# Payload scatters that wait for every batch of four (16 in the edge sums) to have landed

## The chip, the cores and the metric

One core of a Trainium2 chip runs the whole program in one launch. The metric is the device time in microseconds, the median of several executions without a profiler. The profile is one more execution of the same program, recorded by the hardware profiler.

## What is computed

Four blocks are applied one after the other to 6250 nodes with 256 features; each adds its result to its input. The edges are a list of pairs (source, destination).

```python
x = x + gnn0(layernorm(x), edges, edge_attr_32)   # mean of relu(attr @ W_time) over the edges of a node, dense adapter
x = x + ffn0(layernorm(x))                        # router, 6 experts of 3 layers, the best 2 per node
x = x + gnn1(layernorm(x), edges)                 # 2 layers of graph attention, 106250 edges
x = x + ffn1(layernorm(x), ffn_edges)             # router by graph attention (131072 edges), 4 experts, the best 2
```

The graph attention of a layer is

```python
e = leaky_relu(el[src] + er[dst]); ex = exp(e - segment_max(e, dst)[dst])
out = segment_sum(hp[src] * (ex / segment_sum(ex, dst)[dst])[:, None], dst)
```

## The kernel before

The program is a row of stages, each a method with a block of its own; a stage begins when all engines have left the one before. In order: `setup`, `sorts`, `edge_sums`, `norm_T`, `adapter`, `ln_stats`, `norm_T`, `router0`, `gates`, `experts`, `ln_stats`, then twice `gat_tables` and `attention`, then `finish`, `ln_stats`, `norm_T`, `router_tables`, `attention`, `last_experts`.

`sorts` works out for every edge at which place it stands once the edges are grouped by destination, and writes the edge attributes to these places in DRAM (`attr_sorted`, L274: 832 indirect DMAs from GpSimd). Of two further lists it keeps the places (`pos`) and a payload of 16 bytes per edge (`pay`) in SBUF: 832 columns of 128 edges for list 1 and 1024 for list 2. These payloads must stand sorted in DRAM (`pay_sorted`) before the `attention` that reads them back. One indirect DMA of GpSimd (a scatter, L449) writes one column: 128 rows of 16 bytes, each to its own place. That makes 1856 scatters.

They are not a stage of their own. They are shared out over the stages between `sorts` and the attentions, where GpSimd has nothing else to do: each stage gets a list `scatter=[(list, first column, end)]`, and its GpSimd program consists of `scatter_pool` for that list and nothing more. The counts, in order of the stages:

| Stage | Scatters |
|---|---|
| edge_sums | 384 |
| norm_T (three times) | 56 each |
| adapter | 148 |
| ln_stats (three times) | 24 each |
| router0 | 56 |
| gates | 14 |
| experts | 94 of list 1, then 560 of list 2 |
| gat_tables (twice) | 104 each |
| finish | 68 |
| router_tables | 84 |

In `scatter_pool` (L437 to L455) the scatters go out in batches of `AHEAD` = 16 that count their landings on two semaphores in turn. Before a batch, GpSimd waits until the batch before last has landed, so that up to 32 scatters are under way and the batch just issued may still be landing. At the end it waits for both semaphores. Every stage has its own pair, and no other engine waits for a scatter: what it holds up is the end of its stage, and so the start of the next.

The gathers of `attention` (L790: 928 for each of the first two, 1216 for the third) are indirect DMAs of GpSimd too. Before the gathers of a group, GpSimd waits for `s_U`, TensorE's count of finished groups.

Of the kernel before, what the change touches and what calls it, by code (L numbers as in the profile page):

```python
# [49 lines left out]
STEP = 7  # L50
RING = 8
DRING = 8
AHEAD = 16
SLOPE = 0.2
BIG = 2.0 ** 100
NX0, NX1 = 6, 4
# [27 lines left out]
class Kernel:  # L84
# [345 lines left out]
                self.stats(dve, c, st, dl, var, s_var, s_std)  # L430


    def scatter_slots(self, sem, g, lo, hi):

        return dict(g=g, lo=lo, hi=hi, done=sem.pool(2))

    def scatter_pool(self, pool, s):  # L437


        g, lo, hi, done = s["g"], s["lo"], s["hi"], s["done"]  # L440
        out = self.pay_sorted[g]
        last = pool.to_reg(out.shape[0] - 1)
        issued = [0, 0]
        for n in range(hi - lo):
            j = n // AHEAD % 2
            if n % AHEAD == 0 and issued[j]:
                pool.wait_ge(done[j], 16 * issued[j])
            issued[j] += 1
            pool.indirect_dma_start(  # L449
                out=out, out_offset=bass.IndirectOffsetOnAxis(ap=self.pos[g][:, lo + n:lo + n + 1], axis=0),  # L450
                in_=self.pay[g][:, lo + n, :], in_offset=None,
                bounds_check=last, oob_is_err=False).then_inc(done[j], 16)
        for j in range(2):
            if issued[j]:
                pool.wait_ge(done[j], 16 * issued[j])  # L455


    def stats(self, dve, c, st, dl, var, s_var, s_std):
# [1772 lines left out]
def program(nc, ins, out):  # L2231
    i = ins
    with ExitStack() as keep:
        k = Kernel(nc, ins, out)
        k.setup(keep)
        k.sorts()
        with nc.sbuf_tensor("acc0", [P, NB, AD + 1], F32) as acc0:
            k.edge_sums(acc0, scatter=[(1, 0, 384)])
            with nc.sbuf_tensor("XT0", [P, KT, NB * P], F32) as XT:
                k.norm_T(XT, scatter=[(1, 384, 440)])  # L2240
                k.adapter(XT, acc0, scatter=[(1, 440, 588)])
        k.ln_stats(scatter=[(1, 588, 612)])
        with nc.sbuf_tensor("XT1", [P, KT, NB * P], F32) as XT, nc.sbuf_tensor("LG0", [P, NB, NX0], F32) as LG, \
                nc.sbuf_tensor("g0", [P, NB, NX0], F32) as g:
            k.norm_T(XT, scatter=[(1, 612, 668)])
            k.router0(XT, LG, scatter=[(1, 668, 724)])
            k.gates(LG, g, NX0, True, scatter=[(1, 724, 738)])
            k.experts(XT, g, [(i["L0_ffn_expert_w1"], i["L0_ffn_expert_b1"], ACT.Relu),
                              (i["L0_ffn_expert_w2"], i["L0_ffn_expert_b2"], ACT.Relu),
                              (i["L0_ffn_expert_w3"], i["L0_ffn_expert_b3"])], NX0, scatter=[(1, 738, ET), (2, 0, 560)])  # L2250
        k.ln_stats(scatter=[(2, 560, 584)])
        with nc.sbuf_tensor("acc1", [P, NB, D + 1], F32) as acc, nc.sbuf_tensor("m1", [P, NB, 1], F32) as m, \
                nc.sbuf_tensor("adst1", [P, NB, 1], F32) as adst:
            for layer in range(2):
                k.gat_tables(layer, acc, m, adst, scatter=[(2, 584 + 104 * layer, 688 + 104 * layer)])
                k.attention(1, 1, D + 1, k.tab_gat, acc, m, adst)
            k.finish(acc, i["L1_gnn_bias"][1:2, :], scatter=[(2, 792, 860)])
        k.ln_stats(scatter=[(2, 860, 884)])
        with nc.sbuf_tensor("XT2", [P, KT, NB * P], F32) as XT:
            k.norm_T(XT, scatter=[(2, 884, 940)])  # L2260
            with nc.sbuf_tensor("acc2", [P, NB, 3 * HEADS * FH1], F32) as acc, \
                    nc.sbuf_tensor("m2", [P, NB, HEADS], F32) as m, nc.sbuf_tensor("adst2", [P, NB, HEADS], F32) as adst, \
                    nc.sbuf_tensor("W1", [P, NX1, KT, HID], F32) as W1, nc.sbuf_tensor("W2", [P, NX1, HID // P, D], F32) as W2, \
                    nc.sbuf_tensor("B1", [P, NX1, HID // P], F32) as B1:
                w, b = i["L1_ffn_W1"], i["L1_ffn_W2"]
                loads = [(W1[:, e, :, :], w[e].rearrange("(k p) m -> p k m", p=P)) for e in range(NX1)]
                loads += [(W2[:, e, :, :], b[e].rearrange("(k p) m -> p k m", p=P)) for e in range(NX1)]
                loads.append((B1[:, :, :], i["L1_ffn_b1"].rearrange("e (m p) -> p e m", p=P)))
                y = nc.dram_tensor("expert_parts", (PRE * P, NX1 * CB * D), F32).ap()
                dense = dict(XT=XT, W1=W1, W2=W2, B1=B1, y=y, loads=loads)  # L2270
                k.router_tables(XT, acc, m, adst, scatter=[(2, 940, FT)])
                k.attention(2, HEADS, HEADS * FH1, k.tab_rt, acc, m, adst, dense)
                k.last_experts(XT, acc, dense)
# [23 lines left out]
```

## Time and profile before

| What | us |
|---|---|
| Median of 3 executions | 8325.13 |
| Lowest and highest | 8316.30, 8344.27 |
| Span of the profiled execution, first to last instruction | 10342.3 |

For the profiled execution there is no time beside its span. The span is 2017 us longer than the median of the executions without a profiler, and this gap has to be kept in mind with every row below.

By the trace the stages begin and end as follows. "Scatters" is from the first to the end of the last one that GpSimd issues in the stage, "others" is the end of the last instruction of any other engine, both in us from the start of the span.

| Stage | Begins | Scatters until | Others until |
|---|---|---|---|
| sorts | 3 | (1388, attributes) | 1310 |
| edge_sums | 1413 | 1924 | 2310 |
| norm_T | 2312 | 2383 | 2399 |
| adapter | 2400 | 2600 | 2637 |
| ln_stats | 2638 | 2669 | 2657 |
| norm_T | 2674 | 2746 | 2761 |
| router0 | 2763 | 2834 | 2867 |
| gates | 2868 | 2887 | 2880 |
| experts | 2891 | 3778 | 4450 |
| ln_stats | 4452 | 4482 | 4470 |
| gat_tables | 4487 | 4620 | 4719 |
| attention | 4722 | (6106, gathers) | 6138 |
| gat_tables | 6140 | 6276 | 6361 |
| attention | 6364 | (7749, gathers) | 7782 |
| finish | 7784 | 7884 | 7859 |
| ln_stats | 7892 | 7923 | 7910 |
| norm_T | 7927 | 7999 | 8015 |
| router_tables | 8016 | 8123 | 8164 |
| attention | 8180 | (10091, gathers) | 10121 |
| last_experts | 10123 | | 10338 |

To read it: the later of the last two columns ends the stage. A scatter is shown as a busy stretch of GpSimd (POOL) while its descriptors are made; the data lands after that.

### The profile page before, as it was taken

The page shows a single profiled execution, that of the slowest core. Times are in us where ns is not written, and L with a number is a line of the kernel's source. Part 1 is how long each engine was busy: PE and PEld are TensorE (multiplying, and loading weights), DVE is VectorE, ACT ScalarE, POOL GpSimd, SP SyncE. Part 2 cuts the span into 40 slices and gives each one's busy share as a digit, 9 for nine tenths or more (in the row PEclk, how much of TensorE's full clock was granted, in tenths as well). Part 3 has the DMA queues.
Part 4 walks back from the last instruction along what each step waited for, and adds up shares of the span by engine and source line. Part 5 has one row for each costly group of instructions (what it writes and reads, how often), then busy time and mean ns, then how long its engine had stood idle before and what let it go on. Part 6 is the DMA issues. An engine that isn't in the chain of part 4 may idle for free. (4 is left out here: it accounts for less than half of the span.)

```text
span 10342.3 us, 116779 instructions
## 1 busy us (share of the span) xinstructions
PE 5494.0 (53%) x22610; PEld 3209.3 (31%) x22610; DVE 5413.1 (52%) x18917; ACT 3566.1 (34%) x11436; POOL 5780.8 (56%) x5781
## 2 busy tenths in 40 slices
PE   0000001593221149936777764777771388888897
PEld 0000000481110025523444432444441134434445
DVE  8577400492200012226666654666663287788777
ACT  0000000241000012214666642666661176666662
POOL 3787767307567740044666654666666566566650
PEclk9999975795565569967878876888885577677658
DMA  4111100010000000002333321333330111111113
GB/s 128 24 21 22 23 11 4 22 40 3 2 23 1 1 1 0 0 12 84 91 91 91 92 64 57 92 91 91 92 89 2 25 23 22 23 23 24 22 22 101
DMA packets 476242, 426.24 MB, mean 41 GB/s; under 512 B 269726, under 2 KB 409876, under 8 KB 475668
## 3 DMA queue, kind: packets, MB, share of 16 engines
q0 software_dynamic: 214016, 282.62, 11.8%
q1 hardware_dynamic: 224020, 120.13, 4.3%
q10 hardware_dynamic: 37632, 17.48, 0.7%
q8 instruction: 159, 2.61, 0.1%
q14 instruction: 415, 3.40, 0.1%
HBM read 341.50 MB, written 78.72 MB: 41 GB/s over the span
## 5 line engine op out<-in xcount | busy, mean ns | idle before, releaser
L449 POOL DMA_INDIRECT pay_sorted<-pay,pos x1856 | 1883.4, 1015 | 1893.7 <-PEq L1217 721.2
L790 POOL DMA_INDIRECT G<-tab_gat,pay x1856 | 1770.4, 954 | 1187.3 <-issue 465.5
L790 POOL DMA_INDIRECT G<-tab_rt,pay x1216 | 1151.5, 947 | 816.0 <-PE pLU L867 353.0
L864 PE MATMUL pU<-G,PM 128*128 128x257 f32 x3712 | 1269.6, 475 | 324.3 <-ACT PM L961 191.4
L274 POOL DMA_INDIRECT attr_sorted<-rows,pos x832 | 972.9, 1169 | 411.3 <-issue 253.4
L864 PEld LDWEIGHTS pU<-G,PM 128*128 128x128 f32 x3712 | 808.2, 241 | 485.4 <-ACT PM L961 235.6
L1679 DVE TENSOR_TENSOR t<-pO,BL 128x1024 f32<-128x1024 f32 (+1 forms) x78 | 90.7, 1163 | 1345.3 <-remote 871.0
L1078 DVE TENSOR_REDUCE mt<-pW 128x4 f32<-128x2048 f32 x304 | 695.4, 2287 | 163.5 <-issue 77.6
L810 PE MATMUL pA<-identb,G 128*20 128x128 bf16 (+1 forms) x3072 | 438.6, 250 | 477.8 <-issue 202.8
L1663 ACT ACTIVATE H<-pH,B 128x512 f32<-128x512 f32 (+1 forms) x312 | 206.6, 663 | 1364.6 <-remote 691.2
L909 ACT ACTIVATE aT<-pA 20x256 bf16<-20x256 bf16 (+1 forms) x1232 | 512.3, 416 | 457.1 <-PE pA L810 170.5
L1626 PE MATMUL pO<-WL,H 128*128 128x256 f32 x1176 | 288.8, 401 | 573.6 <-issue 345.7
L1167 DVE SCALAR_TENSOR_TENSOR e<-e 128x256 f32<-128x256 f32 x928 | 396.2, 427 | 366.8 <-ACT e L955 292.8
L955 ACT ACTIVATE e<-pW,adst 128x256 f32<-128x256 f32 x928 | 438.0, 472 | 298.8 <-DVE mt L1051 209.4
L961 ACT ACTIVATE PM<-pP 128x256 f32<-128x256 f32 x928 | 339.6, 366 | 574.0 <-PE pP L836 380.6
L810 PEld LDWEIGHTS pA<-identb,G 128*20 128x20 bf16 (+1 forms) x3072 | 190.2, 98 | 1081.4 <-issue 1064.6
L836 PE MATMUL pP<-ident,PT 128*128 128x128 f32 x1856 | 490.6, 354 | 0.0
L1051 DVE TENSOR_REDUCE mt<-pW 128x1 f32<-128x256 f32 x928 | 389.6, 420 | 189.5 <-PE pW L820 136.9
L1175 DVE SCALAR_TENSOR_TENSOR acc<-acc,alpha,pU 128x257 f32 x928 | 442.5, 477 | 77.8 <-PE pU L864 41.2
L970 ACT ACTIVATE PT<-e,bias 128x256 f32<-128x256 f32 x928 | 458.3, 494 | 0.7 <-DVE e L1167 0.7
L322 ACT ACTIVATE rows<-lo 128x16 f32<-128x16 f32 x52 | 11.6, 229 | 1291.8 <-DMA attr_sorted<-rows,pos 1223.4
L593 PE MATMUL pT<-ident,attr 128*128 128x128 f32 x256 | 76.0, 297 | 708.5 <-issue 674.4
(324 smaller groups left out, 12213.3 us busy)
## 6 DMA issues: line engine op xcount, KB each, us to landing
pay_sorted<-pay,pos POOLq DMA_INDIRECT x1856
G<-tab_gat,pay POOLq DMA_INDIRECT x1856
G<-tab_rt,pay POOLq DMA_INDIRECT x1216
expert_parts<-pos SPq DMA_DIRECT2D x144, 128.0 KB
yl<-expert_parts SPq DMA_DIRECT2D x36, 512.0 KB, 4.0
attr_sorted<-zattr SPq DMA_DIRECT2D x1, 16896.0 KB, 53.2
rows<-attr_sorted ACTq DMA_DIRECT2D x256, 66.0 KB
attr_sorted<-rows,pos POOLq DMA_INDIRECT x832
```

Source lines behind the costliest of these rows:

```text
L274: pool.indirect_dma_start(out=self.attr_sorted, out_offset=bass.IndirectOffsetOnAxis(ap=pos0[:, t:t + 1], axis=0), in_=rows[:, j, k, :], i ...
L449: pool.indirect_dma_start(out=out, out_offset=bass.IndirectOffsetOnAxis(ap=self.pos[g][:, lo + n:lo + n + 1], axis=0), in_=self.pay[g][:, ...
L790: pool.indirect_dma_start(out=G[:, j, k, 0:R], out_offset=None, in_=table, in_offset=bass.IndirectOffsetOnAxis(ap=pay[:, g % (2 * PART), k ...
L810: ins = nc.tensor.transpose(pA[j % len(pA)][:, k * P:(k + 1) * P], parts[:, k, 0:ROWS], self.identb[:, :])
L836: ins = nc.tensor.transpose(pP[j % 2][:, k * P:(k + 1) * P], PT[:, j % 2, k * P:(k + 1) * P], self.ident[:, :])
L864: ins = nc.tensor.matmul(u[:, 0:F], PM[:, j % 2, k * P:(k + 1) * P], G[:, j, k, 0:F], start=(k == 0), stop=(k == K - 1))
L909: a.activation(aT[:, j % 2, :], pA[j % len(pA)][:, 0:K * P], ACT.Copy).then_inc(s_aT, 1)
L955: a.activation(e[:, j % 2, :], pW[j % 2][:, 0:K * P], ACT.Identity, bias=ad).then_inc(s_y, 1)
L970: a.activation(PT[:, s, :], e[:, s, :], ACT.Exp, bias=bias[:, j % 4:j % 4 + 1]).then_inc(s_PT, 1)
L1078: v.tensor_reduce(mt, pW[:, :, :], AX.X, ALU.max).then_inc(s_max, 1)
L1167: v.scalar_tensor_tensor(e[:, j % 2, :], e[:, j % 2, :], SLOPE, e[:, j % 2, :], ALU.mult, ALU.max).then_inc(s_e, 1)
L1175: v.scalar_tensor_tensor(ac, ac, alpha[:, j, 0:1], pU[j % 2][:, 0:F], ALU.mult, ALU.add).then_inc(s_acc, 1)
```

## The change

`scatter_pool` now counts all landings of its list on one semaphore. Before every batch but the first it waits until all scatters issued so far have landed. A batch has four scatters, and 16 in `edge_sums`. The wait at the end stays. Nothing else is changed: the lists, their order and the share of each stage are the same, and so are the instructions of the other engines.

```diff
-AHEAD = 16
...
-    def scatter_slots(self, sem, g, lo, hi):
-
-        return dict(g=g, lo=lo, hi=hi, done=sem.pool(2))
+    def scatter_slots(self, sem, g, lo, hi, batch=4):
+
+        return dict(g=g, lo=lo, hi=hi, batch=batch, done=sem.pool(1)[0])
...
-        g, lo, hi, done = s["g"], s["lo"], s["hi"], s["done"]
+        g, lo, hi, batch, done = s["g"], s["lo"], s["hi"], s["batch"], s["done"]
         out = self.pay_sorted[g]
         last = pool.to_reg(out.shape[0] - 1)
-        issued = [0, 0]
         for n in range(hi - lo):
-            j = n // AHEAD % 2
-            if n % AHEAD == 0 and issued[j]:
-                pool.wait_ge(done[j], 16 * issued[j])
-            issued[j] += 1
+            if n and n % batch == 0:
+                pool.wait_ge(done, 16 * n)
             pool.indirect_dma_start(
...
-                bounds_check=last, oob_is_err=False).then_inc(done[j], 16)
-        for j in range(2):
-            if issued[j]:
-                pool.wait_ge(done[j], 16 * issued[j])
+                bounds_check=last, oob_is_err=False).then_inc(done, 16)
+        pool.wait_ge(done, 16 * (hi - lo))
...
-            k.edge_sums(acc0, scatter=[(1, 0, 384)])
+            k.edge_sums(acc0, scatter=[(1, 0, 384, 16)])
```

What stands on GpSimd at the beginning of `experts`, before the change (`s_indirect18` and `s_indirect19` are the two semaphores of the list; a wait is part of the DMA instruction that follows it):

```order
L449 DMA pay_sorted<-pay,pos 118784x4 x32
L449 DMA pay_sorted<-pay,pos 118784x4 [waits s_indirect18]
L449 DMA pay_sorted<-pay,pos 118784x4 x15
L449 DMA pay_sorted<-pay,pos 118784x4 [waits s_indirect19]
L449 DMA pay_sorted<-pay,pos 118784x4 x15
```

The same place after the change, with the one semaphore of the list:

```order
L445 DMA pay_sorted<-pay,pos 118784x4 x4
L445 DMA pay_sorted<-pay,pos 118784x4 [waits s_indirect11]
L445 DMA pay_sorted<-pay,pos 118784x4 x3
L445 DMA pay_sorted<-pay,pos 118784x4 [waits s_indirect11]
L445 DMA pay_sorted<-pay,pos 118784x4 x3
```

No scatter has moved; the waits stand closer, and each is for the scatter right before it.

## Rows read from the trace of the kernel before

**Rows 1.** The page, its head: span and number of instructions.
```profile
span 10342.3 us, 116779 instructions
```

**Rows 2.** Windows: stretch, its length, busy us and (instructions) by engine; clock, DMA share, GB/s.
```profile
core 0: us, PE busy (x) PEld busy (x) DVE busy (x) ACT busy (x) POOL busy (x), PEclk, DMA share, GB/s
1413.00:1924.00 511.00, 59.55 (x205) 46.93 (x205) 35.98 (x143) 13.05 (x38) 383.26 (x384) 0.52 0.04 6
1924.00:2309.00 385.00, 354.39 (x2610) 329.76 (x2611) 336.27 (x1651) 164.03 (x474) 0.46 (x1) 0.95 0.17 40
2312.00:2383.00 71.00, 13.64 (x64) 11.58 (x64) 10.95 (x31) 6.52 (x12) 54.23 (x56) 0.55 0.03 2
2383.00:2399.00 16.00, 6.00 (x34) 5.11 (x34) 5.85 (x17) 6.75 (x14) 0.28 (x1) 0.66 0.00 0
2400.00:2600.00 200.00, 88.71 (x180) 37.51 (x180) 55.65 (x110) 19.57 (x30) 153.83 (x148) 0.60 0.03 3
2600.00:2637.00 37.00, 22.82 (x45) 9.80 (x45) 14.71 (x29) 4.91 (x9) 0.01 (x1) 0.55 0.00 0
2762.00:2834.00 72.00, 20.10 (x52) 10.08 (x52) 0.73 (x4) 2.75 (x4) 54.52 (x56) 0.62 0.03 4
2834.00:2867.00 33.00, 24.74 (x98) 14.02 (x98) 1.63 (x9) 5.87 (x9) 0.02 (x1) 0.89 0.00 0
2911.00:3778.00 867.00, 162.16 (x344) 86.34 (x344) 26.71 (x46) 28.86 (x42) 660.05 (x638) 0.58 0.02 1
3778.00:4450.00 672.00, 648.56 (x2080) 389.16 (x2080) 187.12 (x327) 177.74 (x270) 0.19 (x1) 0.98 0.00 0
4487.00:4620.00 133.00, 21.82 (x80) 17.62 (x80) 18.86 (x79) 6.34 (x9) 101.39 (x104) 0.58 0.07 15
4620.00:4719.00 99.00, 56.23 (x214) 44.50 (x214) 61.31 (x273) 19.29 (x30) 0.43 (x1) 0.74 0.15 54
8016.00:8123.00 107.00, 30.75 (x86) 12.88 (x87) 1.35 (x6) 4.11 (x7) 81.69 (x84) 0.58 0.03 2
8123.00:8162.00 39.00, 17.92 (x65) 7.71 (x63) 9.37 (x21) 3.20 (x6) 0.09 (x1) 0.76 0.00 0
```

**Rows 3.** Timeline of experts while scatters run: start, us, instruction, [idle before it].
```profile
3263.02 6.04 PE L1626 MATMUL pO<-WL,H 128*128 128x256 f32 x16 [58.26 <-issue]
...
3329.47 1.23 DVE L1679 TENSOR_TENSOR t<-pO,BL 128x1024 f32<-128x1024 f32 x1 [86.67 <-remote]
```

**Rows 4.** Timeline of ACT in the first norm_T, whose scatters begin at 2312.
```profile
2316.46 1.09 ACT L1288 ACTIVATE XT<-pX 128x512 f32<-128x512 f32 x2 [0.62 <-PE pX L1277]
...
2366.14 1.08 ACT L1288 ACTIVATE XT<-pX 128x512 f32 x2 [20.61 <-remote]
```

**Rows 5.** Windows of the three attentions, and their sum.
```profile
4724.00:6138.00 1414.00, 1038.28 (x4177) 602.65 (x4177) 935.16 (x3739) 842.14 (x3250) 885.84 (x928) 0.80 0.33 89
8183.00:10120.00 1937.00, 1587.62 (x6897) 759.77 (x6897) 1518.66 (x6423) 1289.34 (x3742) 1151.24 (x1216) 0.69 0.14 24
sum 4767.00, PE 3658.98 PEld 1963.38 DVE 3386.61 ACT 2972.45 POOL 2921.63; mean PE 1219.66 PEld 654.46 DVE 1128.87 ACT 990.82 POOL 973.88
```

**Rows 6.** Timeline of POOL in experts, where list 2 follows list 1.
```profile
3008.16 0.97 POOL L449 DMA_INDIRECT pay_sorted<-pay,pos  x1 [0.30 <-issue]
3009.44 0.97 POOL L449 DMA_INDIRECT pay_sorted<-pay,pos  x1 [0.30 <-issue]
3012.38 0.97 POOL L449 DMA_INDIRECT pay_sorted<-pay,pos  x1 [1.97 <-DMA pay_sorted<-pay,pos]
```

**Rows 7.** Timeline of sorts: the 16th attribute scatter, and ACT, which waits for it.
```profile
186.50 0.97 POOL L274 DMA_INDIRECT attr_sorted<-rows,pos  x1 [0.30 <-issue]
...
188.70 0.23 ACT L322 ACTIVATE rows<-lo 128x16 f32<-128x16 f32 x1 [115.26 <-DMA attr_sorted<-rows,pos]
```

**Rows 8.** Timeline of POOL in the first attention.
```profile
4844.36 0.95 POOL L790 DMA_INDIRECT G<-tab_gat,pay  x1 [0.30 <-issue]
4847.04 0.95 POOL L790 DMA_INDIRECT G<-tab_gat,pay  x1 [1.73 <-remote]
```

**Rows 9.** Timeline of the second ln_stats: last work of DVE, last scatter.
```profile
4469.61 0.47 DVE L474 RECIPROCAL rstd<-dl 128x49 f32<-128x49 f32 x1 [0.31 <-issue]
...
4481.49 0.97 POOL L449 DMA_INDIRECT pay_sorted<-pay,pos  x1 [0.30 <-issue]
```

**Rows 10.** Window of POOL in finish, from the end of VectorE's work.
```profile
7859.00:7884.00 25.00, 19.21 (x20) 0.50 0.03 1
```

## The prediction, made before the changed kernel ran

> **What bounds the kernel now.** I read the table of stages first, since a scatter can only cost time where it ends its stage. In the profiled execution it does so in few places: the three ln_stats (the last scatter starts 12 us after VectorE's last work, [rows 9]), gates, and finish [rows 10]. Everywhere else the other engines are last, in edge_sums by 385 us and in experts by 672 us [rows 2]. Read like this, nearly all scatters are covered.
>
> The windows say why that cover can't be trusted. While 384 scatters run in edge_sums, TensorE does 205 matmuls in 511 us; in the 385 us after them it does 2610. In experts it is 344 in 867 us against 2080 in 672 us [rows 2]. So the other engines don't work beside the scatters, they come after them. The timeline shows the form of this delay. TensorE executes 16 matmuls of experts by 3269.06, at their ordinary pace, but VectorE, which waits for them, starts only at 3329.47 [rows 3]. The work is done on time and its completion is seen 60 us late. It also builds up: in norm_T the first transposes come through while scatters already run (ACT idle 0.62 us), 50 us later ACT waits 20.61 us for the same work [rows 4]. And it doesn't go by the size of the matmul: edge_sums passes 205 in 511 us, 2.5 us each, experts 344 in 867 us, 2.5 us each, though the latter have four to eight times the columns. This is how a queue with one entry per instruction would behave, if it drained slowly while GpSimd issues back to back. The profiled execution leaves one record per instruction, 116779 in all [rows 1]; a timed run leaves none. That the queue is the profiler's is my inference, and the next step tests it.
>
> **Does this delay exist in the timed runs?** The span is 10342 us [rows 1], the median 8325. Suppose the delay were there in full. Then all stages but the attentions keep their profiled length, 10342 - 4767 = 5575 us, and the attentions would have to fit in 8325 - 5575 = 2750 us. VectorE alone is busy for 3387 us in them [rows 5], so that can't be. Suppose it is absent. Then each stage is as long as the longer of its scatters and of the other engines' work at the pace of the windows without scatters [rows 2]: edge_sums 2815 matmuls x 385/2610 = 415 us against 511 of scatters, experts 2424 x 672/2080 = 783 against 887 (from 2891 to 3778), gat_tables 294 x 99/214 = 136 against 133, adapter 225 x 37/45 = 185 against 200, router0 150 x 33/98 = 51 against 72, norm_T 98 x 16/34 = 46 against 71, router_tables 151 x 39/65 = 91 and a store of 17 after it, 108 against 107. The stages shrink by some 385 (edge_sums) + 672 (experts) + 175 (gat_tables) + 37 (adapter) + 33 (router0) + 45 (norm_T) + 40 (router_tables) = 1387 us, to a total of 8955, and the attentions have to give the other 630. Their gathers bound them from below by 3072 x 1.25 = 3840 us (0.95 and a gap of 0.30, [rows 8]), so up to 927 are there to be given. It fits. I take it that in the timed runs the scatters are the longest chain of nearly every stage that has them.
>
> The Trainium skill (SBUF — State Buffer, Who interferes with whom) states that TensorE and ScalarE never wait on another engine for memory. The trace has TensorE's completions 60 us late beside scatters, but its matmuls themselves at ordinary pace, so it doesn't contradict the page on the memory. By the page's rule the cover of the profile is unreal and the sum below holds; if instead the late completions were real in the timed runs too, it would be the sum of rival 1.
>
> **What a wait costs.** Now a scatter starts 0.30 us after the end of the one before [rows 6]. The old waits cost nothing, since what they wait for has landed some 20 us before. After the change each starts only when its predecessor has landed. Two rows bound that. List 2 in experts begins after a full drain: the gap is 1.97 us, 1.67 more than 0.30, with a register load in it [rows 6]. In sorts the 16th scatter ends at 187.47 and ACT, waiting for it, starts at 188.70 [rows 7]: 1.23 us, 0.93 more than 0.30. The new waits are part of the DMA instruction and have no register load, so I take a value near the lower row, 1.0 us, and keep 0.93 and 1.67 for the range. Queued behind the waiting instruction is only the rest of the list; who waits for that is the end of the stage. A cost below nothing has no row for it where scatters end a stage: no scatter gets shorter.
>
> **The sum.** A list of N has (N-1)/4 waits, rounded down, and 23 in edge_sums. At 1.0 us each:
> edge_sums 23; three norm_T of 13, 39; adapter 36; three ln_stats of 5, 15; router0 13; gates 3; experts 23 + 139 = 162; two gat_tables of 25, less the 3 by which the others are later, 44; finish 16; router_tables 20, less 1 and some for the store, 18. Together 369 us of 377 waits. That the one semaphore takes the place of two costs and saves nothing, one wait at a stage's end that has been met by then. The other engines' cover for these waits is already 96 us short of the scatters in edge_sums and 104 in experts, so nothing hides them there. 8325 + 369 = 8694 us. With 0.93 a wait it is 8668, with 1.67 it is 8947. What is late next after the waits is still the scatter list in each of these stages.
>
> **Rivals.**
> 1. The late completions are real in the timed runs, and the pauses don't help them. Then the table of stages holds: only ln_stats, gates and finish pay, 15 + 3 + 16 = 34 us; norm_T has 15 us of cover for 13, adapter 37 for 36, router0 33 for 13. That gives 8359. For it: the rows, taken at their word. Against it: the 2750 us above.
> 2. Faster. The delay is real, and the pauses let TensorE's completions through. In the attentions GpSimd pauses 1.73 us now and then [rows 8], and there TensorE passes 4177 matmuls in 1414 us beside 928 gathers [rows 5], 4.5 per gather where experts has 0.54 per scatter. If a pause after every four scatters did the same, experts would end with its scatters, 887 + 162 = 1049 us in place of 1559, gat_tables at 158 in place of 231 and 220, router0 at 85 in place of 104; edge_sums, with a pause every 16, would gain some 50. That is 510 + 135 + 19 + 50, less the 34 above and some 20 for adapter and norm_T, 660 us: 7665. It decides from the point at which the delay of experts in the timed runs is over the 162 us of waits. Against it stands the same 2750.
> 3. Slower by more. Each wait costs what the drain between the two lists does, 1.67 us: 8947.
> 4. A scatter goes faster without the profiler, at 0.97 us with no gap. Then the other engines end edge_sums (415 against 372 + 23), adapter, gat_tables and router_tables, and the waits vanish in them; experts pays 634 + 162 - 783 = 13, norm_T 39, router0 13, ln_stats 15, gates 3, finish 7. That is 90 us: 8415. Against it: sorts, attentions and the scatter stages would then all be shorter, and a total well below 8325 would be expected.
> That the change doesn't do what it says I rule out: the order of GpSimd's instructions has a wait at every fourth scatter.
>
> **Chances.** Forecast 0.64, rival 1 0.10, rival 2 0.08, rival 3 0.12, rival 4 0.06. The predicted time is 8694. The range from 8410 to 8950 takes in the forecast with both ends of a wait's price and rivals 3 and 4, 0.82 in all. 0.3% is 25 us, about what a measurement of this kernel can tell from no change. Slower by more than that: forecast, rivals 3 and 4 and most of rival 1, whose 34 us are near the bound, 0.87. Within it 0.05, faster 0.08.
>
> **What the profile of the changed kernel would show.** The price of a wait: every fourth scatter with a gap of 1.2 to 1.4 us before it in place of 0.30; 1.97 would be rival 3. The profiled execution need not grow with the timed one. As its completions are let through in the pauses (rival 2's mechanism, which I expect in the profile only), experts should shrink there towards 1100 us and the span to 9700 to 10000, while the median grows. Span and median going apart is the sharpest sign that the delay belongs to the profiler. What would make the prediction wrong: a median below 8400, or experts in the profile as long as before; then TensorE's delay is not what I take it for.

## The result

The changed kernel takes 8743.79 us (median of 3), the kernel before 8325.13 us. By the medians it is 419 us slower. The ratio is 1.0517 with an interval of 1.0461 to 1.0573, which is 384 to 477 us. The forecast was 8694 us, slower by 369.

The span of its profiled execution is 8742.0 us, the same as its timed median. That is 1600 us below the span of the kernel before in [rows 1], though the kernel is slower. So the profile in front of the prediction can't be compared with this one directly. Profiled once more (first experiment below), the kernel before has a span of 8296.8 us, and all comparisons of profiles from here on are with that one, called the second profile of before.

Windows of the changed kernel, columns as in [rows 2]: edge_sums, experts until its other engines are done, experts from there to its last scatter, the first gat_tables, the first and the third attention.

```profile
core 0: us, PE busy (x) PEld busy (x) DVE busy (x) ACT busy (x) POOL busy (x), PEclk, DMA share, GB/s
1402.00:1928.00 526.00, 382.70 (x2816) 354.52 (x2816) 375.83 (x1793) 176.94 (x512) 374.98 (x382) 0.89 0.17 35
2552.00:3317.00 765.00, 762.92 (x2424) 454.11 (x2424) 213.88 (x372) 206.53 (x312) 475.62 (x482) 1.00 0.02 1
3317.00:3568.00 251.00, 0.00 (x0) 0.00 (x0) 0.48 (x1) 0.00 (x0) 155.60 (x161) 0.51 0.02 1
3624.00:3791.00 167.00, 74.15 (x294) 59.02 (x294) 81.94 (x350) 25.51 (x39) 102.32 (x101) 0.69 0.13 40
3802.00:4987.00 1185.00, 894.30 (x4177) 534.45 (x4177) 940.17 (x3749) 870.20 (x3250) 888.18 (x928) 0.89 0.40 107
...
6768.00:8520.00 1752.00, 1529.68 (x6901) 750.17 (x6901) 1507.03 (x6439) 1280.02 (x3742) 1150.50 (x1216) 0.72 0.15 27
```

In the third row little runs but scatters: TensorE has done all 2424 matmuls of experts at 3317, and the stage goes on for 251 us for its last 161 scatters. In [rows 2] it was the other way round. The second profile of before, the same stages:

```profile
1405.00:1903.00 498.00, 385.17 (x2816) 356.87 (x2816) 376.70 (x1793) 177.04 (x512) 377.21 (x382) 0.91 0.18 37
2438.00:3201.00 763.00, 760.63 (x2424) 453.09 (x2422) 214.15 (x372) 206.57 (x312) 577.36 (x586) 1.00 0.03 2
3201.00:3266.00 65.00, 0.00 (x0) 0.00 (x0) 0.00 (x0) 0.00 (x0) 49.51 (x51) 0.50 0.03 2
3463.00:4653.00 1190.00, 910.34 (x4177) 544.35 (x4177) 941.50 (x3749) 866.45 (x3250) 892.32 (x928) 0.88 0.40 106
...
6340.00:8075.00 1735.00, 1500.08 (x6901) 738.25 (x6901) 1506.62 (x6437) 1279.52 (x3742) 1153.52 (x1216) 0.74 0.15 27
```

Before the change, too, experts ends with scatters alone, for 65 us. TensorE works at the same pace in both (763 and 765 us for the same matmuls), so the drains (waits until all scatters issued so far have landed) hold nobody up but the list itself.

The price of a drain, from the timeline of GpSimd in experts of the changed kernel; it answers to [rows 6]:

```profile
2559.42 0.97 POOL L445 DMA_INDIRECT pay_sorted<-pay,pos  x1 [1.41 <-DMA pay_sorted<-pay,pos]
2560.70 0.97 POOL L445 DMA_INDIRECT pay_sorted<-pay,pos  x1 [0.30 <-issue]
2561.97 0.97 POOL L445 DMA_INDIRECT pay_sorted<-pay,pos  x1 [0.30 <-issue]
2563.25 0.97 POOL L445 DMA_INDIRECT pay_sorted<-pay,pos  x1 [0.30 <-issue]
2565.62 0.97 POOL L445 DMA_INDIRECT pay_sorted<-pay,pos  x1 [1.41 <-DMA pay_sorted<-pay,pos]
```

Every fourth scatter starts 1.41 us after the end of the one before it in place of 0.30, so a drain costs 1.11 us. That is less than a scatter's time to land. A scatter lands 2.1 us after its start (view of its line in the changed kernel; us):

```profile
DMA to landing us min/median/max: 2.1/2.1/13.9
```

Of these 2.1 us GpSimd is busy for 0.97 with the scatter itself. With a drain the next one starts 0.97 + 1.41 = 2.38 us after it, without one 0.97 + 0.30 = 1.27 us. What is paid is the difference.

The list of what GpSimd waited for ahead of a scatter (us in total, times), the changed kernel first:

```profile
L445 POOL DMA_INDIRECT pay_sorted<-pay,pos x1856: 964/971/11827, 1402.3 to 6758.0; - x186
its engine sat idle before it (us, times) until:
  DMA pay_sorted<-pay,pos: 556.0, 377
  issue: 467.7, 1464
```

The second profile of before:

```profile
L449 POOL DMA_INDIRECT pay_sorted<-pay,pos x1856: 967/974/12859, 1405.2 to 6329.3; - x186
its engine sat idle before it (us, times) until:
  issue: 571.3, 1840
...
  DMA pay_sorted<-pay,pos: 2.0, 1
```

The 377 waits for a DMA in the first view are 376 drains and the wait between the two lists in experts, which stands in the second view too; the 377th drain, 2.98 us long, is counted under "issue". Their mean is 1.47 us, a little over the usual 1.41: 20 of the drains are longer than 1.6 us, and one in router_tables is 9.37. Idle time ahead of scatters grows from 571 + 2 = 573 to 556 + 468 = 1024 us, by 450. The span grows by 8742.0 - 8296.8 = 445 us. By stage, from the first instruction of any engine in one to the first in the next, in the two traces:

| Stages | Second profile of before | Changed | Difference | Forecast |
|---|---|---|---|---|
| edge_sums | 508 | 535 | 27 | 23 |
| norm_T, three | 238 | 279 | 42 | 39 |
| adapter | 210 | 250 | 40 | 36 |
| ln_stats, three | 106 | 122 | 16 | 15 |
| router0 | 78 | 92 | 14 | 13 |
| gates | 23 | 26 | 3 | 3 |
| experts | 861 | 1047 | 186 | 162 |
| gat_tables, two | 302 | 367 | 65 | 44 |
| finish | 107 | 124 | 17 | 16 |
| router_tables | 118 | 147 | 29 | 18 |
| attention, three | 4122 | 4132 | 10 | 0 |

The stages with scatters take 2550.7 us before and 2989.2 after, so the drains cost 438.5 us, 1.16 each. This sum is steadier than the total: in the third profile of the unchanged kernel (below) it is 2548.7 us, while the attentions, in which nothing was changed, take 4151 us there against 4122.

### The profile page after: what moved, and what is told of

Read it like the earlier page. It is cut to its first block and busy times, and to the rows that moved or that the text cites. A ratio compares the mean times of both kernels' runs of the same rounds, so it can differ in the third digit from the quotient of the medians.

```text
span 8742.0 us, 116764 instructions
## 1 busy us (share of the span) xinstructions
PE 5018.9 (57%) x22610; PEld 2984.9 (34%) x22610; DVE 5412.6 (62%) x18917; ACT 3621.7 (41%) x11436; POOL 5759.8 (66%) x5781
## 5 line engine op out<-in xcount | busy, mean ns | idle before, releaser
L445 POOL DMA_INDIRECT pay_sorted<-pay,pos x1856 | 1851.8, 998 | 1145.5 <-DMA pay_sorted<-pay,pos 556.0
L858 PE MATMUL pU<-G,PM 128*128 128x257 f32 x3712 | 1072.6, 416 | 3.1 <-DVE acc L1169 3.1
L858 PEld LDWEIGHTS pU<-G,PM 128*128 128x128 f32 x3712 | 703.6, 211 | 70.8 <-ACT PM L955 3.6
L883 PE MATMUL pE<-W,pay 128*128 128x256 f32 x1152 | 449.9, 559 | 0.0
L830 PE MATMUL pP<-ident,PT 128*128 128x128 f32 x1856 | 442.0, 323 | 0.0
L822 PE MATMUL pW<-aT,sel 28*128 28x512 bf16 x1216 | 404.1, 462 | 12.7 <-DVE mt L1072 12.7
```

The source lines that it names most:

```text
L445: pool.indirect_dma_start(out=out, out_offset=bass.IndirectOffsetOnAxis(ap=self.pos[g][:, lo + n:lo + n + 1], axis=0), in_=self.pay[g][:, ...
L830: ins = nc.tensor.transpose(pP[j % 2][:, k * P:(k + 1) * P], PT[:, j % 2, k * P:(k + 1) * P], self.ident[:, :])
L858: ins = nc.tensor.matmul(u[:, 0:F], PM[:, j % 2, k * P:(k + 1) * P], G[:, j, k, 0:F], start=(k == 0), stop=(k == K - 1))
L883: ins = nc.tensor.matmul(pE[:, 0:D], hid[u % 2][:, k, i * P:(i + 1) * P], W2[:, x, k, :], start=(k == 0), stop=(k == HID // P - 1))
```

## The experiments

Ratios are to the kernel before on the same chip, with their intervals.

**The kernel before, profiled again.** No edit.

> The kernel before, unchanged, profiled once more. Timed, every theory expects no change (8325 us). The theories differ on the profile. Theory A, the late completions belong to that one profiled execution and to nothing in the program: the span comes out near the timed run, 8330 us, experts takes about 890 us and the first attention about 1185 us (as in the profile of the changed kernel, where the attentions are untouched code). Theory B, scatters that are never drained set them off for the rest of the run: the span is again near 10300 us, experts again 1560 us, and the attention, which stands behind undrained scatters, 1415 us.

Measured: 8338.73 us, ratio 0.9991 (0.9962 to 1.0021), span 8296.8 us. Experts is 861 us (table above) and the first attention 1190, against 1561 (2891 to 4452 in the table of stages of the first profile) and 1414 [rows 5]. Theory A holds. VectorE in experts now waits for TensorE's matmuls for as long as these take, where [rows 3] had it wait 86.67 us (second profile of before, timeline of DVE; start, us, instruction, idle before it):

```profile
2608.64 1.22 DVE L1679 TENSOR_TENSOR t<-pO,BL 128x1024 f32<-128x1024 f32 x1 [7.28 <-PE pO L1626]
```

So the program alone doesn't bring the late completions about; they belong to its first profiled execution.

**Twice the profile again.** A third profile of the unchanged kernel, and one whose waits would allow far more scatters under way:

```diff
-AHEAD = 16
+AHEAD = 64
```

> The kernel before, unchanged, profiled a third time. If the late completions of its first profile come back in some profiled executions, this is a further draw: span 8300 us if they don't, 10300 us if they do. If they are rare, 8300 is expected by either theory and settles nothing more than their frequency.

> The kernel before with AHEAD = 64: up to 128 scatters may be under way by its waits, so in most stages GpSimd waits for nothing but the end. Theory (waits for what has long landed cost nothing, and back to back scatters set off no delay): 8325 us and a span of 8300 us. Rival (many undrained scatters can set off the late completions, and 32 under way is the edge of it): the span is again near 10300 us, with experts at 1560 us.

Measured: spans of 8320.4 and 8317.3 us, times of 8322.16 and 8319.11 us from one execution each (the kernel before beside them 8351.63). No late completions in either. ahead64 says little about how many scatters it takes to set them off, though: a scatter lands 2.1 us after its start and the next starts 1.27 us after it, so that with either `AHEAD` mostly two are under way, far below the 32 or 128 that the waits allow. Of the profiled executions of this study, the one in front of the prediction alone has late completions. What caused them there stays open; it wasn't seen again and so couldn't be taken apart.

**Batches of 16 everywhere.**

```diff
-    def scatter_slots(self, sem, g, lo, hi, batch=4):
+    def scatter_slots(self, sem, g, lo, hi, batch=16):
```

> The changed kernel with batches of 16 in all stages in place of 4. Theory (each drain costs what the profile of the changed kernel shows, a gap of 1.40 in place of 0.30 us, because the scatters are the longest chain of their stage): 107 waits x 1.10 = 118 us, less 6 of cover in gat_tables, so 8437 us, ratio 1.013. Rival (the cost lies in keeping fewer scatters under way at all times, not in the number of drains): near the changed kernel, 8744 us.

**Batches of 2.**

```diff
-    def scatter_slots(self, sem, g, lo, hi, batch=4):
+    def scatter_slots(self, sem, g, lo, hi, batch=2):
```

> The changed kernel with batches of 2 in place of 4 (16 in edge_sums as before). Theory: 744 waits x 1.10 = 818 us over the kernel before, 9140 us, ratio 1.098; twice the waits, twice the loss. Rival (part of the 419 us of the change is a fixed cost, such as one semaphore in place of two): less than twice, 8950 to 9050 us.

Measured: 8487.61 us, ratio 1.0159 (1.0106 to 1.0212), and 9187.42 us, ratio 1.1007 (1.0951 to 1.1064). What GpSimd waited for ahead of a scatter, with batches of 16 (107 drains and the wait between the lists):

```profile
  issue: 550.4, 1733
  DMA pay_sorted<-pay,pos: 167.4, 108
```

With batches of 2:

```profile
  DMA pay_sorted<-pay,pos: 1083.3, 743
  issue: 356.3, 1098
```

| Kernel | Drains | Median slower by, us | Stages with scatters longer by, us | Per drain, by stages, us |
|---|---|---|---|---|
| Batches of 16 | 107 | 8487.61 - 8343.79 = 144 | 143 | 1.34 |
| Changed kernel | 377 | 8743.79 - 8325.13 = 419 | 439 | 1.16 |
| Batches of 2 | 744 | 9187.42 - 8343.79 = 844 | 850 | 1.14 |

The loss follows the number of drains. The rival of a fixed cost expected less than twice the loss of the changed kernel for batches of 2, and got twice (844 against 2 x 419 = 838). The batches of 16 lost 32 us more than the 112 expected. The interval of their ratio is as wide as 88 us and takes in the expected 1.013, but the trace shows where most of it lies: one drain in router_tables lasts 12.07 us, and there is a small cost that isn't per drain. In the second profile of before GpSimd pauses for 1.6 to 1.9 us at about every 113th scatter of a long list; in all three kernels with drains most of these pauses are 3.0 us. Eight of them make about 10 us. Why they grow stays open.

**At least as many waits, but none for the batch just issued.**

```diff
-AHEAD = 16
+AHEAD = 4
```

> The kernel before with AHEAD = 4 in place of 16: as many waits on the semaphores as in batches of four, but each for the batch before last, so up to 8 scatters are under way and GpSimd never waits for the one just issued. Theory: what is waited for has landed 5 us before, so a wait costs nothing: 8325 us, ratio 1.000 (within 0.3%). Rival (the waiting instruction itself is what costs): part of the 1.10 us per wait comes back, 8400 us or more.

Measured: 8327.52 us, ratio 0.9979 (0.9946 to 1.0012). What GpSimd waited for ahead of a scatter:

```profile
  issue: 575.3, 1839
...
  DMA pay_sorted<-pay,pos: 10.0, 3
```

Batches are of four in edge_sums too, so there are more waits than in the changed kernel, and there is no loss. So neither the waiting instruction nor the size of the batch costs anything that these runs can tell; what costs is that the wait is for the scatter just issued.

**The drains in experts alone.**

```diff
-                              (i["L0_ffn_expert_w3"], i["L0_ffn_expert_b3"])], NX0, scatter=[(1, 738, ET), (2, 0, 560)])
+                              (i["L0_ffn_expert_w3"], i["L0_ffn_expert_b3"])], NX0, scatter=[(1, 738, ET, 4), (2, 0, 560, 4)])
```

(`scatter_slots` takes a batch size; where it is given, `scatter_pool` waits on one semaphore as in the changed kernel, else as in the kernel before.)

> The kernel before with the drains of four in experts alone, all other stages as before. Theory (the scatter list ends the stage by some 75 us over the other engines, so its 162 drains of 1.10 us all count): 178 us more, 8503 us, ratio 1.021. Rival (the profile of the kernel before, taken at its word: experts ends 672 us after its last scatter): nothing, ratio 1.000.

Measured: 8506.98 us against 8331.35, ratio 1.0214 (1.0175 to 1.0253): 176 us for 162 drains by the medians, within 146 to 211. Its windows of experts, beside the other engines and after them:

```profile
2438.00:3202.00 764.00, 761.70 (x2424) 453.46 (x2422) 214.36 (x372) 206.61 (x312) 471.09 (x478) 1.00 0.02 1
3202.00:3461.00 259.00, 0.00 (x0) 0.00 (x0) 0.00 (x0) 0.00 (x0) 161.44 (x166) 0.50 0.02 1
```

The list ends 259 us after the other engines, where it was 65. From the first matmul on the stage takes 1023 us against 763 + 65 = 828, so by the trace the drains cost 195 us. The rival, the profile in front of the prediction taken at its word, expected none of it.

**Cover for the drains of experts.** 360 scatters are left out of experts, from the kernel before and from the changed one. 360 columns of payloads are then never written, and the two kernels are read for their time alone:

```diff
-                              ... NX0, scatter=[(1, 738, ET), (2, 0, 560)])
+                              ... NX0, scatter=[(1, 738, ET), (2, 0, 200)])
```

> The kernel before with 360 of the 560 list 2 scatters of experts left out (columns 200 to 559 of list 2 are never written), so that experts has 294 scatters: 294 x 1.28 = 376 us beside 765 us of the other engines' work. Theory: the stage falls back to its other engines, 65 to 75 us less than the kernel before: 8255 us, ratio 0.992. Rival (by the profile of the kernel before, in which the other engines work only after the scatters): 360 x 1.28 = 461 us less, 7865 us, ratio 0.945.

> The changed kernel with the same 360 scatters left out. Its experts has 294 scatters with 72 drains, 376 + 79 = 455 us, under the 765 us of the other engines. Theory: these drains are covered and cost nothing, only the 215 of the other stages do, 237 us over the trimmed kernel before: 8495 us, ratio 1.020. Rival (a drain costs wherever it stands, for instance by holding up other engines): the 72 are added, 79 us more, 8574 us, ratio 1.030.

Measured: 8261.82 us, ratio 0.9898 (0.9849 to 0.9946), and 8498.20 us, ratio 1.0199 (1.0144 to 1.0255). Experts without the drains, from its first matmul to the end of its other engines, and with them:

```profile
2431.00:3196.00 765.00, 762.72 (x2424) 453.87 (x2424) 214.15 (x372) 206.54 (x312) 274.19 (x278) 1.00 0.01 1
```

```profile
2559.00:3323.00 764.00, 761.14 (x2424) 453.36 (x2423) 214.41 (x372) 206.56 (x312) 278.61 (x283) 1.00 0.01 1
```

Both stages end with TensorE's 2424 matmuls, and from their first scatter to the next stage both take 786 to 787 us. The 72 drains vanish behind the matmuls: between the two kernels lie 236 us where at 1.10 us each the 215 drains outside experts make 237 and all 287 would make 316. And leaving out 360 scatters gains 70 us, not the 461 that they take, since the other engines end the stage from there on. This is the rule by which the change cost what it did, seen from both sides.

## Why the prediction was right, and where it wasn't

**The bound: right.** The step that carried the forecast was to set aside the cover that [rows 2] show, because 2750 us would not have held the attentions with 3387 us of VectorE's work [rows 5]. The second profile of before bears it out: its attentions take 1190 + 1190 + 1735 = 4115 us where the working left them 8325 - (8955 - 4767) = 4137, and each stage with scatters ends with them, by 7 us in gates and by 94 in edge_sums.

**The cause of the late completions: not shown, and not as described.** The working put them down to back to back scatters filling a queue of the profiler. Back to back scatters alone don't do it: three further profiles have them (the kernel before twice, and ahead64) and no late completions. Of the rest only this is shown, that the late completions come from one profiled execution and not from the program, and that the timed runs were free of them. That it was the profiler's queue stays a guess. Two statements about the changed kernel's profile hung on it and fell: a span of 9700 to 10000 us (measured: 8742), and span and median going apart (they agree). A third, experts shrinking towards 1100 us, came near (1047) by luck. The step that failed there is the argument from the pauses: they removed no delay. Experts without any pauses is free of it too (861 us in the second profile of before, 1561 in the first), and so are the attentions, where nothing was changed (1185 us against 1414 in [rows 5]).

**What a drain costs: the term that was too small.** 1.0 us was taken, with 0.93 and 1.67 as bounds; the usual drain is 1.11 by its gap. It lies near the lower row, [rows 7], as argued. Between the two lists, where there is a register load as well, the gap is 1.90 us in the changed kernel too, against 1.41 at a drain. 377 x 0.11 makes 41 of the 50 us by which the forecast was short of the median.

**The count: right.** 377 drains were counted and 377 are in the trace.

**The cover: less than assumed.** In gat_tables the other engines were taken to be last by 3 us and in router_tables by 1 and a store. In the second profile of before they end 21 us (3430.6 against 3451.7) and, the second time, 15 us ahead of the scatters in gat_tables; in router_tables they end 48 us ahead (6282.6 against 6330.3), and the store has landed 34 us ahead, at 6295.9. Their pace had been read from windows of the first profile: it gave 136 us for the other engines in a gat_tables, where they take 117, and 91 in router_tables, where they take 61. So no drain is covered there, and the 8 us taken off the 377 for cover are the rest of the 50.

**What the sum did not have.** By the traces the loss is 439 us and not 419, still within the interval of the timed runs. The excess over 377 x 1.11 is mostly in drains that last longer than usual, one of 9.37 us among them, and in the longer pauses at every 113th scatter. That 41 and 8 us make up the 50 so nearly is in part luck, since the median itself has an interval of 93 us.

**The rivals.** Rival 1 (34 us) and rival 2 (faster) rested on late completions in the timed runs. Both are excluded by the 419 us, and experts4 shows that experts alone pays 176 us. Rival 3 (1.67 us) is excluded by the gap of 1.41. Rival 4 (scatters without their gap of 0.30 us in timed runs) is excluded by the profiled executions, which show the gap and take as long as the timed ones.

The Trainium skill (SBUF — State Buffer, Who interferes with whom), by which TensorE waits for no other engine's use of the memory, agrees with the second profile of before: 763 us for TensorE's 2424 matmuls beside scatters, 765 with drains between them, and 765 in trim_before, where the scatters end halfway.

## What to carry to other kernels

On an engine that does nothing else but issue, a wait for the transfer just issued costs each time about what is left of its landing once it is issued (here 1.11 us, of 2.1 from start to landing); a wait for the batch before last costs nothing. With two semaphores in turn, a batch could be as small as four here. Whether such waits matter is decided by which list of work ends the stage; if the profile's span is far from the timed median, check that reading against the timed total before believing any cover, and profile again if you can.

## What was unexpected of the hardware

One profiled execution of a program can be 24% longer than its timed runs (10342.3 against 8325.13 us) with TensorE's completions seen up to tens of microseconds late, while two further profiles of the same kernel take 8296.8 and 8320.4 us. In that trace the scatters' own rows still held (0.97 us with 0.30 between in both), but waits for TensorE, idle times and which engine ended a stage did not.

In experts, scatters of GpSimd and the other engines' work run side by side with no loss that the traces can tell. The same stretch of the stage in the third profile of before, with scatters, and in trim_before, whose scatters have ended by then:

```profile
2800.00:3190.00 390.00, 390.00 (x1267) 234.86 (x1266) 112.86 (x197) 106.75 (x164) 294.81 (x299) 1.00 0.03 1
```

```profile
2800.00:3190.00 390.00, 390.00 (x1268) 234.75 (x1267) 112.77 (x197) 106.77 (x164) 0.00 (x0) 1.00 0.00 0
```

TensorE does 1267 matmuls beside 299 scatters and 1268 beside none.
